# Moving the state-space block from one instruction stream to the other in a fused two-layer sequence kernel, with another assignment of PSUM banks

## The reference, cut to what matters

```
x  = L0_attn_x                                  # 16 x 512 x 128
xn = layernorm(x)
s  = scan_forward(xn) + scan_backward(xn)       # selective scan, 16 states each: 32 scans of 512 steps
g  = silu(top-2-weighted 4-wide MLP(xn))
x1 = x + s * g
xn = layernorm(x1)
s  = state_space(xn)     # q = rope(W_in x); rmsnorm; 4-tap conv and silu; 4 heads of 64, 128 states;
                         # y = chunked scan + D x; rmsnorm(y * silu(z)); W_out; + q
h  = xn
for layer in 2:          # local attention: 8 heads, window 64, looks one window back
    h = h + attention(shift(h)) @ wo
    h = h + gated_gelu_mlp(layernorm(shift(h)))
out = x1 + s * silu(h)
```

## Time and profile before

| | |
|---|---|
| time, median of 3 runs (lowest, highest) | 4470.81 us (4470.54, 4471.91) |
| the profiled execution: time, span | 4473.03 us, 4471.2 us |
| granted TensorE clock, mean | 0.923 of full speed |
| busy: PE, DVE, ACT, POOL | 77%, 56%, 56%, 38% |
| DMA | 20.5 MB, x and out 256 KB each per sequence |

### The profile page before, as it was taken

How to read it: one execution, slowest core, us unless ns; L and a number is a source line. 1 busy time by engine, 2 the same in 40 slices (tenths; PEclk the granted TensorE clock), 3 DMA queues, 4 the chain that set the end, 5 groups by cost and what they waited for, 6 DMA issues and landing times. The chain is left out here.

```text
span 4471.2 us, 55299 instructions
## 1 busy us (share of the span) xinstructions
PE 3462.7 (77%) x16160; PEld 1873.6 (42%) x16160; DVE 2481.5 (56%) x4239; ACT 2513.2 (56%) x5798; POOL 1718.4 (38%) x1428
## 2 busy tenths in 40 slices
PE   5787778877878788787777778778787787878776
PEld 1344344444444444344443444434444444444443
DVE  6565654646556465564655646565464655646433
ACT  4455556555656555555654555556565555655554
POOL 2253442524425254252533425344252442525332
PEclk9798998989999899998999989999998999989998
DMA  1000000000000000000000000000000000000000
GB/s 77 3 1 1 5 1 5 1 1 6 1 6 1 1 5 1 6 1 6 1 1 6 1 6 1 1 6 1 6 1 1 6 1 6 1 1 3 1 3 3
DMA packets 18390, 20.53 MB, mean 5 GB/s; under 512 B 768, under 2 KB 17152, under 8 KB 17792
## 3 DMA queue, kind: packets, MB, share of 16 engines
q1 hardware_dynamic: 18048, 16.44, 1.1%
HBM read 12.24 MB, written 4.19 MB: 4 GB/s over the span
## 5 line engine op out<-in xcount | busy, mean ns | idle before, releaser
L1393 POOL TENSOR_TENSOR hc<-hst,Cs 128x512 f32<-128x512 f32 x512 | 649.4, 1268 | 1721.2 <-DVE hst L1165 1696.1
L1165 DVE TENSOR_TENSOR_SCAN hst<-dA,bank 128x512 f32<-128x512 f32 x512 | 625.0, 1221 | 337.0 <-ACT dA L862 150.3
L518 PE MATMUL bank<-W,xs 128*128 128x512 f32 x960 | 474.6, 620 | 128.8 <-DVE tmp L1305 126.8
L494 PE MATMUL bank<-hc,C 128*128 128x512 f32 x1024 | 553.9, 624 | 0.8 <-POOL hc L1393 0.7
L506 PE MATMUL bank<-parts,sel 96*128 96x512 bf16 x1024 | 363.4, 410 | 219.1 <-DVE hst L1165 193.5
L1157 DVE TENSOR_TENSOR bank<-u,bank 128x512 f32<-128x512 f32 x512 | 351.9, 687 | 322.7 <-PE bank L506 293.0
L868 ACT COPY Cs<-bank 128x512 f32<-128x512 f32 x512 | 298.5, 583 | 351.8 <-PE bank L506 351.2
L1454 POOL TENSOR_TENSOR oT<-tmp 128x512 f32<-128x512 f32 x256 | 324.3, 1267 | 329.8 <-PE bank L670 168.9
L993 ACT ACTIVATE Pm<-bank,mx 128x128 f32<-128x128 f32 x1024 | 362.3, 369 | 118.0 <-DVE mx L1325 118.0
L1469 POOL TENSOR_TENSOR Pm<-Pm,rinv 128x512 f32<-128x512 f32 x256 | 266.0, 1039 | 376.4 <-DVE rinv L1318 358.9
L862 ACT ACTIVATE dA<-delta,neg_a 128x512 f32<-128x512 f32 x512 | 371.3, 725 | 4.9 <-issue 4.1
(11 more groups left out here) (221 smaller groups left out, 6085.2 us busy)
## 6 DMA issues: line engine op xcount, KB each, us to landing
W<-wpack SPq DMA_DIRECT2D x1, 4498.0 KB, 13.6
x_tok<-x SPq DMA_DIRECT2D x16, 256.0 KB, 3.6
out<-xa SPq DMA_DIRECT2D x16, 256.0 KB, 3.5
rot<-tables SPq DMA_DIRECT2D x2, 512.0 KB, 16.2
wc_f<-taps SPq DMA_DIRECT2D x1, 1024.0 KB, 19.5
C<-cpack SPq DMA_DIRECT2D x1, 721.0 KB, 14.8
Pm<-mask SPq DMA_DIRECT2D x1, 320.0 KB, 15.1
tmp<-rowpack SPq DMA_DIRECT2D x1, 256.0 KB, 17.4
```

The lines of the kernel that those rows point to most:

```text
L494: mm(y_acc[:, :], ident, hc[:, k % 2, :], start=(k == 0), stop=(k == 2 * NS - 1))\
L518: mm(b[:, :], weights, rhs, start=True, stop=True).then_inc(full(ring, job), 1)
L1165: v.tensor_tensor_scan(o, a, b, 0.0, ALU.mult, ALU.add).then_inc(sem("a_h"), 1)
L1393: g_.tensor_tensor(hc[:, k % 2, :], hst[:, k % 2, :], Cs[:, k % 2, :], ALU.mult)\
```

## The change

Mamba becomes a stage of its own, `mamba(i)`, and joins stream A behind head(i); stream B is the two layers only. Its slots, its instructions, and their order among themselves stay; `LAYER` goes from 11 to 1. Sequence 0's mamba now runs in the part before the woven passes, and sequence 15's no longer in the part behind them.

- Buffers. The layers' kT, oT, vt, Pm, PT, on, tmp1, tmp2 and rsB are in use by the layers of the other sequence now, so mamba works in buffers of scan and prologue that are dead between them (hst, hc, bx, gate, delta, u, dA, xc, Cs, dlow). New waits say so: ACT waits for `m_sm1` of the sequence before in prologue's slot 4, DVE for `t_xs` of the one before in head and for `m_sm` in mamba's last step. One buffer, `smb`, is new.
- Start of `stage_b`: ACT copies xn2 into the shifted xs0 (two copies), POOL adds the residual (`m_sm`). The copy x1b, and the finish of the sequence before (transposes, copy, store) move into layer 0, slots 2 to 4.
- PSUM. A bank is assigned by use: a job takes the ring's bank that was used longest ago, but in the scan `B{k}` has bank k mod 2 and `C{k}` always the third. So C{k} waits for ACT's copy of C{k-1}, and B{k} for scan k-2.
- `CUT` is 0, so that scan's slots are 0 to 31 as before.

With LAYER_SLOTS = 20, the new map puts scan steps 0 and 1 beside B's slot 0, steps 2 to 21 beside the 15 slots of layer 0's units, steps 22 to 31 and the end of the scan beside its FFN, head and mamba (19 slots) beside the 15 slots of layer 1's units, and the prologue of the next sequence beside the last FFN.

```diff
@@ jobs: mamba's go from ring B to ring A, behind head's
-B_JOBS = ([("ab0", "m_ld", 1)] + [(f"ab{q}", "m_ea", q) for q in range(1, NT)]
+A_JOBS += ([("ab0", "m_ld", 1)] + [(f"ab{q}", "m_ea", q) for q in range(1, NT)]
...
+B_JOBS = []
@@ slots
+CUT = 0
 SCAN = 0
-A_END = SCAN + 2 * NS
+A_END = SCAN + 2 * NS - CUT
 HEAD = A_END + 1
-PRO = HEAD + 8
-A_SLOTS = PRO + 9
-LAYER = 11
+MAMBA = HEAD + 8
+PRO = MAMBA + 11
+SCAN1 = PRO + 9
+A_SLOTS = SCAN1 + CUT
+LAYER = 1
-PACE = [(0, 2), (LAYER, 16), (LAYER + UNITS_END, 28), (LAYER + LAYER_SLOTS, HEAD), (LAYER + LAYER_SLOTS + 5, PRO),
-        (LAYER + LAYER_SLOTS + UNITS_END, A_SLOTS - 1), (B_END, A_SLOTS - 1), (B_SLOTS, A_SLOTS)]
+PACE = [(0, 0), (LAYER, 2), (LAYER + UNITS_END, 22), (LAYER + LAYER_SLOTS, HEAD), (LAYER + LAYER_SLOTS + UNITS_END, PRO),
+        (B_END, A_SLOTS - 1), (B_SLOTS, A_SLOTS)]
@@ banks
+SCAN_HOME = {f"{name}{k}": k % 2 if name == "B" else 2 for name in "BC" for k in range(2 * NS)}
+def home(jobs, n):
+    at, order = [], list(range(n))
+    for name, _, _ in jobs:
+        b = SCAN_HOME.get(name, order[0])
+        order.remove(b)
+        order.append(b)
+        at.append(b)
+    return at
@@ place
-            b = n % len(bs)
-            return bs[b], b, n // len(bs), len(range(b, len(jobs), len(bs)))
+            b = homes[ring][n]
+            return bs[b], b, homes[ring][:n].count(b), homes[ring].count(b)
@@ buffers
-        big1 = kT[:, :, :].rearrange("p q (h l) -> p q h l", h=HM)
-        big2 = oT[:, :, :].rearrange("p q (h l) -> p q h l", h=HM)
-        xbc, sz, y3 = vt[:, 0:4], vt[:, 4:6], PT
+        heads_of = [t.rearrange("p (h l) -> p h l", h=HM) for t in
+                    (hst[:, 0, :], hst[:, 1, :], hc[:, 0, :], bx[:, 0, :], bx[:, 1, :], hc[:, 1, :], gate[:, :])]
+        big1, big2 = [None] + heads_of[0:3], heads_of[3:7]
+        xbc = [delta[:, 0, :], delta[:, 1, :], u[:, 0, :], u[:, 1, :]]
+        sz, ysq, y_r, sm1 = dA, u, xc, sm
@@ run
-            alone(chain(prologue(0), scan(0), head(0), prologue(1)))
-            both(chain(scan(1), head(1), prologue(2)), stage_b(0, None))
+            def body(i):
+                return chain(scan(i, CUT, 2 * NS), head(i), mamba(i))
+            alone(chain(ready(0), body(0), ready(1)))
+            both(chain(body(1), ready(2)), stage_b(0, None))
...
-            both(chain(scan(NB - 1), head(NB - 1)), stage_b(NB - 2, NB - 3))
+            both(body(NB - 1), stage_b(NB - 2, NB - 3))
             alone(stage_b(NB - 1, NB - 2))
@@ ACT, start of stage_b
+                yield 0
+                shifted(xs0, xn2, "t_xs", "m_xn", i, 1)
@@ POOL, start of stage_b
+                yield 0
                 pool.wait_ge(*step("m_sm1", i))
+                if later(i):
+                    pool.wait_ge(*before("x2a", i))
-                g_.tensor_tensor(sm[:, :], tmp1[:, 0, :], mq[:, :], ALU.add).then_inc(sem("m_sm"), 1)
+                g_.tensor_tensor(smb[:, :], sm1[:, :], mq[:, :], ALU.add).then_inc(sem("m_sm"), 1)
```

More of the change, by code:

```diff
@@ L394, in finish @@
                 sp.dma_start(dst, xo[:, :].rearrange("p (q d) -> p q d", q=NT)).then_inc(sem("store"), 16)
-            run(sp, prologue, scan, head, stage_b, finish)
+            run(sp, prologue, scan, head, mamba, stage_b, finish)
             sp.wait_ge(sem("store"), NB * 16)
@@ L569, in stage_b @@
                                   start=True, stop=True)
-                    last.then_inc(full("B", f"ab{q}"), 1)
+                    last.then_inc(full("A", f"ab{q}"), 1)
                 pe.wait_ge(*step("m_h", i))
                 for t in range(4):
-                    yield 2 + t
-                    if t == 0 and ended is not None:
-                        finish(ended)
-                    if used("B", f"cx{t}", i):
-                        pe.wait_ge(*vacant("B", f"cx{t}", i))
-                    b = bank("B", f"cx{t}")
+                    yield MAMBA + 2 + t
+                    if used("A", f"cx{t}", i):
+                        pe.wait_ge(*vacant("A", f"cx{t}", i))
+                    b = bank("A", f"cx{t}")
                     for k in range(TAPS):
@@ L722, in stage_b @@
                         n = s - UNIT
+                        if l == 0 and s == 2 and ended is not None:
+                            finish(ended)
                         if s < NT:
@@ L771, in finish @@
                 last.then_inc(sem("xo_full"), 1)
-            run(pe, prologue, scan, head, stage_b, finish)
+            run(pe, prologue, scan, head, mamba, stage_b, finish)
         @block.scalar
@@ L824, in prologue @@
                 yield PRO + 4
+                if later(i):
+                    act.wait_ge(*before("m_sm1", i))
                 for d in range(2):
@@ L853, in prologue, with scan @@
                 tables()
-            def scan(i):
-                yield SCAN
-                act.wait_ge(*step("a_delta", i))
-                for k in range(2 * NS):
-                    yield SCAN + k
+            def scan(i, lo, hi):
+                yield scan_slot(lo)
+                if lo == 0:
+                    act.wait_ge(*step("a_delta", i))
+                for k in range(lo, hi):
+                    yield scan_slot(k)
                     if k >= 2:
@@ L949, in stage_b @@
                         n = s - UNIT
+                        if l == 0 and s == 3:
+                            if ended is not None:
+                                finish(ended)
+                            act.wait_ge(*step("a_x1", i))
+                            nc.scalar.copy(x1b[:, :], x1[:, :]).then_inc(sem("m_x1b"), 1)
                         if s < NT:
@@ L1030, in finish @@
                 nc.scalar.copy(xo[:, :], o_acc[:, :]).then_inc(sem("xo"), 1)
-            run(act, prologue, scan, head, stage_b, finish)
+            run(act, prologue, scan, head, mamba, stage_b, finish)
         @block.vector
@@ L1147, in prologue, with scan @@
                                        op0=ALU.add, op1=ALU.mult).then_inc(sem("a_fo"), 1)
[L1149 to L1153 removed]
+            def scan(i, lo, hi):
+                yield scan_slot(lo)
+                if lo == 0:
+                    dve.wait_ge(*step("a_u", i))
+                for k in range(lo, hi):
+                    yield scan_slot(k)
                     d = k // NS
@@ L1285, in stage_b @@
                     yield at_l
-                    if l == 0:
-                        dve.wait_ge(*step("m_sm", i))
+                    if l == 0 and later(i):
+                        dve.wait_ge(*before("x2", i))
                     for s in range(UNITS_END):
@@ L1361, in finish @@
                 pass
-            run(dve, prologue, scan, head, stage_b, finish)
+            run(dve, prologue, scan, head, mamba, stage_b, finish)
         @block.gpsimd
@@ L1380, in prologue, with scan @@
                     .then_inc(sem("a_parts"), 1)
-                prior.append(step("a_parts", i))
-            def scan(i):
-                prior.clear()
-                for k in range(2 * NS):
-                    yield SCAN + k
+                pool.wait_ge(*step("a_parts", i))
+            def scan(i, lo, hi):
+                if lo == CUT:
+                    prior.clear()
+                for k in range(lo, hi):
+                    yield scan_slot(k)
                     pool.wait_ge(*step("a_h", i, k + 1))
@@ L1473, in finish @@
                 pass
-            run(pool, prologue, scan, head, stage_b, finish)
+            run(pool, prologue, scan, head, mamba, stage_b, finish)
 SETUP = 7 + 4 + 3 + 2 + TAPS + 1 + 2 + len(TABLES) * NL
```

289 lines of the change are left out of this document (148 added, 141 removed).

## The result

The changed kernel takes 4515.38 us (median of four runs, 4510.58 to 4518.87), the kernel before 4471.36 in the same comparison: a ratio of 1.0092, 95% interval 1.0072 to 1.0111. It is slower by 0.9%, outside the spread of the runs, where 4410 us was forecast. The profiled span is 4508.7 us against 4471.2.

What follows compares the result with a forecast made beforehand. No engine is full, so the bound was taken to be how the two streams are woven, stage by stage. -4.3 us a pass, 14 times (-60), and -4 in the last pass brought 4473.03 to 4410 us; range 4350 to 4460.

Steps and rivals of the forecast that it cites:

- The predicted -64 us: Whole profiled execution: -60 us from 14 passes and -4 from the last, taken off 4473.03 us.
- The first stretch and layer 0: First scan to layer 0: 3.4 us in place of 67.4; layer 0's units with 20 steps instead of 12: +13.2.
- The mamba stretch and the prologue: Layer 1's unit 3 to last FFN: 58.2 us for 41.5; last FFN to first scan: 43.5 for 23.9.
- the chief rival: Mamba does not hide beside layer 1's units: unit 3 to FFN 65.6 us (deciding from 62.5), 4520 us; chance 0.27.
- Layer 0's FFN: With ten scan steps instead of four and the scan's end, DVE becomes the bound: 32.0 us against 21.7, +10.3.
- Layer 1 to unit 3: Start of layer 1 to its fourth attention unit: head as before, so left at 46.2 us.
- The last pass and sequence 15: Last pass, without prologue: -4 us; mamba 15 taken away behind the passes, 43.9 us.
- The banks: The new PSUM assignment takes the wait for a scan from C; priced at nothing.
- The bound of 16 us a pass: Most the bank assignment could be worth: half of 504.7 / 16, were all that waiting on the path.
- The net of -4.3 us a pass: Sum for one pass of the loop: -64.0 + 13.2 + 10.3 + 16.7 + 19.5.
- PE's clock: PE's granted clock should not fall at the last FFN; 2.4 GHz there was estimated at 2 us a pass.
- The table load: ACT's next instruction comes 1.28 us after a load starts; the skill's extra 1.38 us drain would make it 4430.

Runs made afterwards that it cites:

- e7: e3 with the end of the scan (last two additions, x1) put behind layer 1's first projections: 4446.38 us, ratio 0.9946 to the kernel before.
- e3: The changed kernel with the head in layer 1's first five slots and mamba in the ten behind: 4466.16 us, ratio 0.9987 to the kernel before.
- e2: The kernel before the change with only the new by-use assignment of PSUM banks: 4422.69 us, ratio 0.9893 to the kernel before.
- e1: The changed kernel with PSUM banks given out in turn again, as before the change: 4722.82 us, ratio 1.0557 to the kernel before.

## Why the prediction was wrong

The predicted -64 us in the profiled execution became +37.5, a difference of 101.5. It is made up of 14 times 6.75 us in the passes (275.4 for 268.6, that is 272.9 less the 4.3 forecast), 94.5; 11.3 from the last pass's first scan to sequence 15's layer 0; and 3.8 the other way in the part ahead (40.1 for 43.9). What is left is under 1 us.

**The first stretch and layer 0: right. The mamba stretch and the prologue: right in sum.** In the mean 3.4 us for 3.4, 85.3 for 85.6, 58.7 for 58.2 and 44.5 for 43.5. The eight extra steps beside layer 0's units cost what they were charged, within 1 us. The 58.2 is in part luck. It had 22.5 + 10.3 = 32.8 us from unit 3 to G's mask, where 2096.37 - 2060.62 = 35.8 were measured, and 25.4 behind the mask, where it took 2118.95 - 2096.37 = 22.6; two errors of 3 us cancel. Of the 25.4, the lone stream's 23.9 had been read up to the layer behind mamba, with POOL's last sum in it, which no longer stands before the FFN. This also settles the chief rival. Its time, 4520, is 5 us from the result, but its mark, over 62.5 us from unit 3 to the FFN, was not met; it would have been right for a wrong reason.

**Layer 0's FFN: +2.6 in the rows, +3.1 in the mean. The waits were mis-sized.** The term had 27.0 us of DVE's work (18.5 + 6.4 + 2.1) and 5.0 of waits: 2.3 for POOL's and PE's part of step 31 and 2.7 for dA. This is the stretch in the changed kernel (length, busy us and count of PE, PEld, DVE, ACT and POOL, granted clock, DMA share, GB/s):

```profile
2252.03:2286.65 34.62, 29.19 (x72) 11.36 (x70) 26.64 (x32) 18.61 (x29) 12.67 (x10) 0.95 0.00 0
```

DVE's work was right, 26.6, and its idle time is 8.0 us instead of 5.0. In the timeline of DVE there is no wait for dA. There is the one for PE's last additions, 3.11 us, and there are 2.6 us for the FFN's own matmuls (0.30, 1.08 and 1.24) and 1.12 for ACT's norm factor, which the term didn't have; the rest are gaps of under 0.6. e7 takes the 3.11 away, but in like passes hands all of it on, so it doesn't show that this wait sets the pass.

**Layer 1 to unit 3: +2.5 in the rows, +2.3 in the mean. The head isn't as before.** This was left at 46.2 because "the head is as before". It isn't: the map gives head and mamba one common slope, and the head's last parts fall behind unit 0's exponentials. I had read the map's end points and not where each slot lands between them. e3 puts the head back and wins 49 us; the whole of layer 1 then takes 104.8 us for the 104.4 forecast, where the changed kernel takes 107.2. How much of this is the head, and how much that mamba starts earlier too, e3 doesn't part.

**The last pass and sequence 15: 11.3 too small.** Mamba 15 was credited with its whole 43.9, though the last FFN's end, the copies and POOL's sum now stand before layer 0 (25.7 us from 4322.41 to 4348.12, for the 20.6 that the credit implied): 5.1. The rest is the FFN's 3.2, units 1.5, and 1.6 and 1.0 in layer 1, less 1.2.

**The banks: priced at nothing, worth 207 us.** Relative to the kernel before nothing was needed in the sum, since the other terms were made as if PE never held a second step back; so the sum stands in spite of it. Its argument for slots with one step ("has run ahead again before the next scores") wasn't refuted: in e2 layer 0's units, with at most one step to a slot, gain nothing. What was passed over is the size of the delay that the text "did not charge" in slots with two steps; it makes or breaks this change (e1). The bound of 16 us a pass held (14.6 in e1). In the kernel before the assignment was also worth 49 us, which as a term of its own would have made the forecast 4361 and the miss larger.

**What was wrong in kind.** The net of -4.3 us a pass was a difference of terms that sum to 124 us in size, each good to 2 or 3 us. Its sign wasn't known, and 0.60 on "faster" was more than it bore. e2 beside the changed kernel says it plainly: with the same banks the kernel that leaves mamba alone has a mean pass of 270.0 us, the other of 275.5. What left the stretch before layer 0, 40.8, came back as 12.1 in layer 0's units, 14.2 in its FFN and 20.0 in layer 1.

**PE's clock: wrong.** The forecast said that it would not fall at the last FFN. Before the change it didn't fall at the FFN's last six matmuls (L763, now L801), which take 2.74 us in every woven pass (here in the pass at 2081.10):

```profile
2095.20 2.74 PE L763 MATMUL bank<-kT,W 128*128 128x512 f32 x6
```

In the changed kernel they take 3.86 to 4.71 us in each of the 14 woven passes that have a prologue beside them. The windows of the changed kernel, with the same columns as above, from the FFN's start to this group, through it, and behind it:

```profile
2118.95:2143.89 24.94, 18.04 (x48) 6.59 (x47) 10.27 (x25) 17.84 (x25) 2.12 (x1) 1.00 0.00 1
2143.89:2148.32 4.43, 4.43 (x8) 1.89 (x7) 0.00 (x0) 0.00 (x0) 0.00 (x0) 0.61 0.00 0
2148.32:2158.98 10.66, 6.28 (x22) 2.81 (x20) 10.30 (x11) 5.75 (x7) 0.00 (x0) 0.94 0.01 3
```

It is 1.00, that is 2.4 GHz, for 24.9 us, and falls just after PE has waited 3.12 us for ACT, in the timeline of PE:

```profile
2142.93 1.13 PE L497 MATMUL bank<-hst,W 128*128 128x512 f32 x2 [3.12 <-ACT hst L883]
2143.89 4.43 PE L801 MATMUL bank<-kT,W 128*128 128x512 f32 x6
```

The Trainium skill, "TensorE: Matmul & The Clock Gate", What's actually happening, calls the throttled state the default that activity releases. The trace agrees with the release: the clock is back at 0.94 while the matmuls go on. The 2 us that I set against my own row for that rule did not come in the changed kernel: the stretch to the first scan took 44.3, not 41.5. In e3's five short passes, where L801 runs at the full clock, it takes 42.2 to 42.5. As an estimate, the slower group costs 4.43 - 2.74 = 1.7 us where it stands, up to 24 us in 14 passes; part of it comes back in layer 0's units (1.2 us in e3, last section), and no run here changes the clock alone. I had also called PE "much idle" where the prologue stands alone; the earlier trace rows has it busy for 23.95 of 30.00 us there.

**The table load.** ACT in the same FFN:

```profile
2129.44 0.58 ACT L861 CAST parts<-bank 96x512 bf16<-96x512 f32 x1 [0.28 <-PE bank L474]
2130.03 1.28 ACT L1062 ACT_TABLE_LOAD   x1
2131.33 1.37 ACT L1062 ACTIVATE on<-bank,W 128x512 f32<-128x512 f32 x2
```

The load starts 0.01 us after the cast's end, and the next activation 1.30 us after the load's start. Of the 168 loads in the changed kernel 133 have no wait behind them, and there the next instruction begins 1.28 to 1.30 us after the load's start. A further drain of 1.38 us, as the Trainium skill has it in "ScalarE: Activation LUTs", What ACT_TABLE_LOAD costs, isn't there, and the measurement decides: a switch costs 1.30 here.

## What to carry to other kernels

Where engines take their work in order and none is full, price a move by what each stretch charges for one more piece, in slots that are full and slots that are empty, and read the map slot by slot; if the terms are ten times the net, give the sign little trust and look for a smaller move instead. Try a change of resources (banks, buffers) apart from a change of order: here the one won 49 us where the whole lost 44, and its worth was 49 us in one order and 207 in the other. Compare means over many passes, and like passes with like: the same stretch differs by 1 to 3 us between passes of one execution here. Work that is small and independent goes beside a block that stands alone: four steps there cost 1.5 us and took 5.2 off the next stretch.
